# Tokens stored and loaded back by chunk, changed parameter and table code, and expert rows gathered into four buffers

## What is computed

```python
S = exp(dt_Lambda[..., None] * t - P_max)              # 128 heads, 64 states, 512 steps
Wc = Wc * (exp(dt_Lambda_neg) - 1) * conj(x) / (x * conj(x) + EPS)   # x = den * Lam
h = einsum("chn,hnl->chl", Wc, S).real                 # the tokenizer: 16 x 128 x 512
h = concat(cls_tok, h)
h = h + scan_layer(layernorm(h))    # z = x W_in; gated recurrence both ways; W_out; layer norm
h = h + moe_ffn0(layernorm(h))      # 8 experts, top 2, hidden 256, and a shared expert of 512
h = h + gla_layer(layernorm(h))     # gated linear attention, 16 heads
h = h + moe_ffn1(layernorm(h))      # 8 experts, top 2, hidden 352, and a shared expert of 1408
```

## Time and profile before

| | us |
|---|---|
| median of 3 runs | 1627.94 |
| lowest, highest | 1627.8, 1629.62 |
| the profiled execution, its own time | 1627.72 |
| its span, first to last instruction | 1625.9 |
| PE busy, in the span | 1398.0 |
| DVE busy | 841.7 |
| POOL busy | 476.5 |
| ACT busy | 368.8 |

### The profile page before, as it was taken

How to read it: one execution, slowest core, us unless ns; L and a number is a source line. 1 busy time by engine, 2 the same in 40 slices (tenths; PEclk the granted TensorE clock), 3 DMA queues, 4 the chain that set the end, 5 groups by cost and what they waited for, 6 DMA issues and landing times.

```text
span 1625.9 us, 21254 instructions
## 1 busy us (share of the span) xinstructions
PE 1398.0 (86%) x6461; PEld 1083.6 (67%) x6462; DVE 841.7 (52%) x1730; ACT 368.8 (23%) x703; POOL 476.5 (29%) x350
## 2 busy tenths in 40 slices
PE   0193685999899999379999899999999988989996
PEld 0193333888544444136777588888888877878885
DVE  7895468755322222464567775555555532333332
ACT  1011204211111111142222312332333111212221
POOL 0390502053134444100111025533333112333332
PEclk9999887999999999778999999999999999999998
DMA  2267002501665555610000303666666587666433
GB/s 54 56 103 161 0 0 76 179 21 33 248 174 97 90 91 94 193 30 1 1 1 1 137 20 127 207 213 221 206 207 203 225 323 241 183 179 175 84 71 45
DMA packets 90596, 193.87 MB, mean 119 GB/s; under 512 B 30128, under 2 KB 34096, under 8 KB 87216
## 3 DMA queue, kind: packets, MB, share of 16 engines
q1 hardware_dynamic: 70448, 151.19, 28.4%
q0 software_dynamic: 20096, 42.02, 14.3%
HBM read 112.24 MB, written 77.87 MB: 117 GB/s over the span
## 4 chain that ended last, share of the span: by engine, by line
PE 74%; DVE 12%; DMA 8%; issue 2%; ACT 1%; SPq 1%; POOL 1%; POOLq 0%; DVEq 0%; ACTq 0%
PE ps L1449 21%; PE ps L1509 19%; PE ps L1570 9%; PE ps L1970 6%; DMA out<-moe_scratch 6%; PE ps L1596 4%; PE ps L401 3%; PE ps L1543 2%; DVE held L454 2%; PE ps L510 2%; PE ps L1942 1%; PE ps L729 1%; PE ps L730 1%; PE ps L1584 1%; PE ps L1995 1%
## 5 line engine op out<-in xcount | busy, mean ns | idle before, releaser
L1509 PE MATMUL ps<-moe_rounded 128*128 128x384 f32 (+2 forms) x1800 | 374.1, 350 | 0.0
L1509 PEld LDWEIGHTS ps<-moe_rounded 128*128 128x128 f32 x1800 | 325.7, 188 | 33.1
L1226 DVE SCALAR_TENSOR_TENSOR held<-ps,moe_scratch,held 128x512 f32<-128x512 f32 (+1 forms) x255 | 187.5, 747 | 178.5 <-PE ps L1449 178.3
L1449 PE MATMUL ps<-moe_expert_parts,moe_rows_parts 128*128 (+1 forms) x1320 | 261.8, 352 | 4.5 <-DVE moe_rows_parts L1234 3.1
L1449 PE MATMUL ps<-moe_rounded 128*128 128x512 f32 (+3 forms) x885 | 239.6, 391 | 8.2 <-DVE moe_rounded L1208 6.1
L1449 PEld LDWEIGHTS ps<-moe_expert_parts,moe_rows_parts 128*128 128x128 f32 (+1 forms) x1320 | 222.2, 192 | 18.6 <-issue 5.3
L1449 PEld LDWEIGHTS ps<-moe_rounded 128*128 128x128 f32 (+2 forms) x885 | 145.3, 170 | 46.7 <-DVE moe_rounded L1208 8.1
L1240 DVE TENSOR_TENSOR moe_scratch<-moe_scratch,ps 128x256 f32<-128x256 f32 (+1 forms) x80 | 37.6, 470 | 230.4 <-ACT moe_scratch L1430 230.4
L1570 PE MATMUL ps<-moe_experts,moe_scratch 128*128 x320 | 145.9, 599 | 1.7 <-ACT moe_scratch L1416 1.1
L1327 POOL TENSOR_TENSOR moe_split_parts<-moe_scratch,moe_split_parts 128x704 fp32r<-128x704 f32 (+2 forms) x48 | 88.3, 1845 | 173.9 <-ACT moe_split_parts L1405 173.8
L1246 DVE TENSOR_SCALAR moe_scratch<-ps,moe_scratch 128x512 f32<-128x512 f32 x80 | 60.0, 751 | 130.6 <-PE ps L1596 56.8
(11 more groups left out here) (295 smaller groups left out, 1630.8 us busy)
## 6 DMA issues: line engine op xcount, KB each, us to landing
moe_expert_parts<-expert_parts SPq DMA_DIRECT2D x8, 3840.0 KB, 14.5
expert_parts<-moe_split_parts SPq DMA_DIRECT2D x32, 704.0 KB, 3.7
moe_scratch<-in_ffn_gate_up SPq DMA_DIRECT2D x32, 352.0 KB, 4.7
xn_rows<-moe_xn SPq DMA_DIRECT2D x2, 4096.0 KB, 12.8
moe_experts<-in_ffn_gate_up SPq DMA_DIRECT2D x8, 1024.0 KB, 11.6
expert_parts<-moe_split_parts SPq DMA_DIRECT2D x8, 1024.0 KB, 4.7
moe_scratch<-in_ffn_sh_gate_up SPq DMA_DIRECT2D x15, 512.0 KB, 3.4
tokens<-sb SPq DMA_DIRECT2D x64, 64.0 KB, 2.3
```

Of the source, the lines that this page charges most:

```text
L1226: v.scalar_tensor_tensor(out=hb[0:rows, t, :], in0=ps[0:rows, ADDED[t % 3], :], scalar=sg[0:rows, t:t + 1], in1=hb[0:rows, t, :], op0=ALU. ...
L1449: mm = t.matmul(out, lhs(k, x), rhs(k, y), start=(k == 0 and i == 0), stop=(k == ks - 1 and i == 2))
L1509: mm = t.matmul(unit_banks(u, m)[j], weights(k, x, j), xT[y][:, k, unit_cols(m)], start=(k == 0 and i == 0), stop=(k == KD - 1 and i == 2))
```

## The change

- Front: one DMA brings all parameters, laid out on the host as 128x186. The loads of x and the scan layer's weights are issued ahead of all else, GpSimd's two `memset`s (`zero`) too.
- The arguments of the sine are made once, and the cosine's come from them by one instruction (`cosine_args`, with a bias of pi/2 in ScalarE). The coefficient steps are merged over numerator and denominator.
- GpSimd waits for the eight table DMAs of the first group only; the four factor DMAs are issued behind `tabr` 2 and behind these eight. The fourth group is spread behind the stores of chunk 0.
- `tokens` is laid out by head. A chunk is stored by two DMAs of 256 KB, one for each bank, and read back by one DMA of 512 KB into the 16 partitions of its heads (`load_chunk`); the last chunk is read back in four quarters. The layer norm starts when all chunks and the first quarter of the last are there.
- ScalarE makes `xn` for the odd tiles (L712 of the new kernel), and the projection of quarter 0, 1, 2 and 3 follows tile 3, 9, 14 and 16.
- Experts: four buffers each for gathered rows and for results; two of each lie in `hb`, so that the first use of these waits for the stores of h (`hst`). `LAG` is 6, a gather waits for the tile four before it, and the loop is over four tiles.

```diff
-    def sync(sp):
...
+    def loads(sp):
+        sp.dma_start(params, d["tok_params"]).then_inc(par_in, 16)
         for w, k in ((wre, 0), (wim, 1)):
             for half in (LO, HI):
...
+        def tables(k):
             frm = LO if k < 2 else HI
             for to, lo, hi in ((R1, re[:, 0], re[:, 0]), (D1, re[:, 1], im[:, 1]), (I1, im[:, 0], im[:, 0]), (D2, ni2, re[:, 1])):
                 spread(to, LO, lo, frm, k, t_in[k])
                 spread(to, HI, hi, frm, k, t_in[k])
-            if k == 0:
-                sp.wait_ge(tabr, 2)
+
...
+        def store(k, b):
+            sp.wait_ge(evac, 2 * k + b + 1)
+            sp.dma_start(h0v[:, k * HC + b * H8:k * HC + (b + 1) * H8, :],
+                         ob[:, k % 2, b * QC:(b + 1) * QC].rearrange("p (h j) -> p h j", j=TJ)).then_inc(stored[k % 2], 16)
+
+        def load_chunk(k):
+
+            sp.wait_ge(stored[k % 2], 16 * 2 * (k // 2 + 1))
+            heads = slice(k * HC, (k + 1) * HC)
+            sp.dma_start(hb[heads, 0:NB, :], rows_of(heads, 0, NB)).then_inc(h_in[0], 16)
...
+        tables(0)
+        sp.wait_ge(tabr, 2)
+        sp.wait_ge(t_in[0], 8 * 16)
+        factors(0)
+        for k in range(1, 3):
+            tables(k)
+            factors(k)
+        last = NHC - 1
         for k in range(NHC):
-            u = k % 2
-            sp.wait_ge(evac, 2 * k + 2)
...
-                             ob[i * NB:(i + 1) * NB, u, :].rearrange("c (h j) -> c h j", j=TJ)).then_inc(stored[u], 16)
-            if k == NHC // 2 + 1:
-                load(LO)
-        load(HI)
+            store(k, 0)
+            if k >= 2:
+                load_chunk(k - 2)
+            store(k, 1)
+            if k == 0:
+                tables(3)
+                factors(3)
+        load_chunk(last - 1)
+        sp.wait_ge(stored[last % 2], 16 * NHC)
+        heads = slice(last * HC, NH)
+        for g in range(NQ):
+            sp.dma_start(hb[heads, 4 * g:4 * g + 4, :], rows_of(heads, 4 * g, 4 * g + 4)).then_inc(h_in[g], 16)
...
-        def args(out, mm, mmk, kk, ph):
-
-            c.link(v.tensor_scalar(out, mmk, ph, MAGIC, ALU.add, ALU.add))
-            c.link(v.scalar_tensor_tensor(out=out, in0=out, scalar=-MAGIC, in1=mm, op0=ALU.add, op1=ALU.subtract))
-            c.link(v.scalar_tensor_tensor(out=out, in0=out, scalar=-ph, in1=kk, op0=ALU.add, op1=ALU.subtract))
-            return v.tensor_scalar(out, out, -0.5, 0.5, ALU.max, ALU.min)
+        def sine_args(out, mm, mmk, kk):
+
+            c.link(v.tensor_scalar(out, mmk, MAGIC, -MAGIC, ALU.add, ALU.add))
+            c.link(v.tensor_tensor(out, out, mm, ALU.subtract))
+            c.link(v.tensor_tensor(out, out, kk, ALU.subtract))
+            c.link(v.tensor_scalar(out, out, -0.5, 0.5, ALU.max, ALU.min))
 
...
+        def cosine_args(out, x):
+
+            return v.scalar_tensor_tensor(out=out, in0=x, scalar=0.25, in1=x, op0=ALU.is_gt, op1=ALU.subtract)
...
+        c.put(v.scalar_tensor_tensor(out=xr, in0=dr, scalar=lam[:, 0:1], in1=w2[:, 0], op0=ALU.mult, op1=ALU.subtract))
+        c.link(v.scalar_tensor_tensor(out=xi, in0=dr, scalar=lam[:, 1:2], in1=w2[:, 1], op0=ALU.mult, op1=ALU.add))
+        c.put(v.tensor_tensor(w2, x2, x2, ALU.mult))
+        c.put(v.tensor_tensor(cc, num, bc(xr.unsqueeze(1), 1, 2), ALU.mult))
...
             if u == 0:
-                g.wait_ge(t_in[k // 2], 12 * 16)
+                g.wait_ge(t_in[k // 2], 12 * 16 if k else 8 * 16)
...
+                    v.wait_ge(h_in[t // NQ], H_LOADED[t // NQ])
                 norm.take_stats(v, hb, t)
                 c.n += 1
             norm.solve_some(v, c, tiles)
+            cols = slice(tiles[0], tiles[-1] + 1)
+            c.put(v.scalar_tensor_tensor(out=nmr[:, cols], in0=norm.mv[:, cols, 0], scalar=-1.0, in1=norm.rstd[:, cols], op0=ALU.mult, op1=ALU.mult))
+            solved.append(c.base + c.n)
             for t in tiles:
-                norm.apply(v, xn, hb, t).then_inc(xr, 1)
+                if t not in BY_SCALAR:
+                    norm.apply(v, xn, hb, t).then_inc(xr, 1)
 
...
-            s.wait_ge(turned, n + 1)
-            turned_out(s, ps[:, TURN_BANKS[n % 4], :], xnT, n).then_inc(tev, 1)
+        for k, tiles in enumerate(GROUPS):
+            s.wait_ge(norm.sem, solved[k])
+            for t in tiles:
+                if t in BY_SCALAR:
+                    s.activation(xn[:, t, :], hb[:, t, :], ACT.Identity, bias=nmr[:, t:t + 1], scale=norm.rstd[:, t:t + 1]).then_inc(xa, 1)
+            for n in tiles:
+                s.wait_ge(turned, n + 1)
...
             if n >= 4:
                 t.wait_ge(tev, n - 3)
             turn_tile(t, ps[:, TURN_BANKS[n % 4], :], xn, n, ident).then_inc(turned, 1)
-            if n == 7:
-                project(slice(0, QC), QC, 2)
+            if n in AFTER:
+                quarter(AFTER[n])
         t.wait_ge(tev, T)
-        for q in range(1, NQ):
-            project(slice(q * QC, (q + 1) * QC), QC, 2 + q)
         project(slice(NCOL, NTOK), NB, 6)
...
+    g_in, G0 = g.rows_gathered, 16 * (NTILE // DEEP) if split_w else 0
+    xg_of = [xg[:, 0], xg[:, 1], hb[:, 0, :], hb[:, 1, :]]
+    ey_of = [ey[:, 0], ey[:, 1], hb[:, 2, :], hb[:, 3, :]]
     tx, txr = sem(name + "_rows_turned"), sem(name + "_rowsT_ready")
     eg, esr, ehr = sem(name + "_e_gate_up"), sem(name + "_e_silu"), sem(name + "_e_hidden")
...
-        def out_rows(t, u):
+        def out_rows(t, x):
+            u = x % 2
             v.wait_ge(ed, D0 + t + 1)
-            if not early(t):
-                v.wait_ge(yst[u], 16 * halves(t))
-            v.tensor_scalar(ey[:, u], ps[:, 6 + u, :], idx[:, bass.ds(t, 1), 1], None, ALU.mult).then_inc(eyr, 1)
+            if not (isinstance(t, int) and t < DEEP):
+                v.wait_ge(yst[u], 16 * halves(t - 2))
+            elif t == 2:
+                v.wait_ge(hst, 16 * (NQ + 1))
+            v.tensor_scalar(ey_of[x], ps[:, 6 + u, :], idx[:, bass.ds(t, 1), 1], None, ALU.mult).then_inc(eyr, 1)
 
...
-    LAG = 4
+    LAG = 6
...
+        def four(i):
+            for k in range(1, DEEP + 1):
+                body(DEEP * i + k, k % DEEP)
+
+        looped(eng, (NTILE - 2) // DEEP, four)
+        for t in range((NTILE - 2) // DEEP * DEEP + 1, NTILE - 1):
+            body(t, t % DEEP)
...
-                if t >= 2:
-                    p.wait_ge(tx, t - 1)
-                p.indirect_dma_start(out=xg[:, t % 2], out_offset=None, in_=xd,
-                                     in_offset=bass.IndirectOffsetOnAxis(ap=idx_u[:, t, 0:1], axis=0)).then_inc(g_in[t % 2], 16)
+                if t >= DEEP:
+                    p.wait_ge(tx, t - DEEP + 1)
+                elif t == 2:
+                    p.wait_ge(hst, 16 * (NQ + 1))
+                p.indirect_dma_start(out=xg_of[t % DEEP], out_offset=None, in_=xd,
+                                     in_offset=bass.IndirectOffsetOnAxis(ap=idx_u[:, t, 0:1], axis=0)).then_inc(g_in[t % DEEP], 16)
             if t >= LAG:
...
+DEEP = 4
...
-        h0 = nc.dram_tensor("tokens", (NB, NH, D), F32).ap()
+        h0 = nc.dram_tensor("tokens", (NH, NB * TI, TJ), F32).ap()
```

188 lines of the change are left out of this document (96 added, 92 removed).

## The result

The changed kernel takes 1603.57 us (1602.61 to 1604.48) where the kernel before took 1628.24, the median of four runs on the same chip: ratio 0.9847, 95% interval 0.983 to 0.9864, so it is 1.5% faster, clear of the spread between runs. The forecast was 1610 with a range of 1596 to 1624. The profiled execution's span went from 1625.9 to 1601.3, -24.6 us, where the sum had -18.0.

What follows compares the result with a forecast made beforehand. TensorE held 74% of the chain that ended last, so the gain had to come from the rest: -1.4 + 1.6 - 5.2 - 13 = -18.0 on 1627.72 us gave 1609.7, say 1610, with a range of 1596 to 1624.

Steps and rivals of the forecast that it cites:

- The front: Start until the coefficient tables are done: 61.6 against 62.98 us, -1.4, with 11.8 lost to six GpSimd products.
- GpSimd hardly disturbs the coefficients: Rival in the front: GpSimd's early products cost VectorE's chain little, 11.8 us more gain, 1598 us; chance 0.14.
- Stores and loads: Tokenizer's end: SyncE's queue bounds it, first statistics at 107.1 + 7.25 L = 144.8 us against 143.2, +1.6.
- L: Tokenizer's loads back: time of one 512 KB load into 16 partitions, taken as 5.2 us.
- L = 2.6: Rival on loads back: as fast as into 64 partitions, evacuations the bound, statistics at 136.6, time 1602; chance 0.15.
- statistics at 137: Sign at the tokenizer's end: first statistics at 137 or past 160 us would mean a wrong L.
- The slower rival: Loads back take 10.3 us each, in proportion to partitions; statistics wait until 181.8, time 1647; chance 0.09.
- Layer norm: First statistics through the first projection: 22.2 + 1.8 + 6.8 + 1.8 + 3.6 + 0.9 = 37.1 us against 42.3, -5.2.
- The rest of the program is untouched: 0: Everything outside the front, loads back, layer norm and expert tiles was forecast to change by 0.
- ffn1: Second expert layer's tiles: -12.3 to result 22, -3.2 from fewer loop edges, 2.5 given back for gathers: -13 us.
- the buffers give nothing: Rival in ffn1: the scatter chain is the bound and moves with the weight loads, time 1623; chance 0.07.
- fully decoupled: Rival in ffn1: gathers and scatters no longer hold each other, 8.1 us more gain, 1602 us; chance 0.10.

Runs made afterwards that it cites:

- e1: Changed kernel, but GpSimd waits for all twelve spreads of the first group, so its first products start behind the coefficients; 1593.29 us, ratio 0.9799 to the kernel before.
- e2: Changed kernel, but GpSimd makes only chunk 0's three products early and chunk 1's wait for the coefficient tables; 1597.17 us, ratio 0.9826 to the kernel before.
- e3: Changed kernel, but all seven whole-chunk loads into 16 partitions follow the last stores; 1629.4 us, ratio 1.0026 to the kernel before.
- e4: Changed kernel, but four loads of 1 MB into 128 partitions behind the last stores replace all chunk loads; 1600.39 us, ratio 0.9852 to the kernel before.
- e6: Changed kernel with the old projection order: quarter 0 behind tile 7, quarters 1 to 3 behind the last tile; 1609.04 us, ratio 0.9883 to the kernel before.
- e9: Changed kernel, but GpSimd adds beta to h only when VectorE's two scans have ended; 1601.83 us, ratio 0.9842 to the kernel before.
- e12: Changed kernel with products behind tables, wide loads at the end, adds behind scans, eight result buffers with varied lag; 1590.38 us, ratio 0.9773 to before.
- e7: Changed kernel with two buffers for gathered rows and results, a two-tile loop and lag four, as before, in both expert layers; 1615.03 us, ratio 0.9912 to before.
- e8: Changed kernel with eight result buffers, a loop over eight tiles and scatters eight tiles behind; 1613.59 us, ratio 0.9914 to the kernel before.

## Why the prediction came out as it did

**The front: -1.4 forecast, -2.9 measured, for the reason given.** Every link was near: first instruction 2.86 (3.5), first spread 34.30 (35.0), GpSimd's first product 40.82 (41.7), tables at 60.06 (61.6). e1 and e2 show that the price of 11.8 us for six products was 11.1. The rival that GpSimd hardly disturbs the coefficients is wrong, since e1 differs from the changed kernel by that alone and its tables end at 48.94. The Trainium skill's rule in "SBUF — State Buffer", section "Who interferes with whom", of an exclusive lock for a whole instruction, agrees with the VectorE rows of 1.86 to 2.45 us. So does the add of 5.49 us beside a scan.

**Stores and loads: the step that failed.** "I take 5.2" for L was 4.6 to 4.7 (e3), and the 2.5 taken for a store was too much too: store and load of a chunk together took 6.0 to 6.3 us, not 7.7, so a store cost some 1.6. Under 7.11 the queue is not the bound, so 107.1 + 7.25 L does not set the statistics; with L = 4.7 it would give 141.2, and they stood at 137.51. What set them is the case that the forecast gave to L = 2.6 only: the last evacuation, and then the last store and load, 10.8 us where 8.4 was reckoned. The last store and the quarter load each had a narrow load in the queue ahead: the store landed 0.8 us behind the load of chunk 5, the quarter 1.2 behind that of chunk 6. In e4, which has neither, the same stretch took 7.6. The sign "statistics at 137", which was to mean a wrong L, came true, but the bound was wrong more than L. The sum has a slip here too: 144.8 is a time from the start of the span, so +1.6 holds the gain of the tables already, and adding -1.4 to it counts that twice. Counted once, the forecast would have been 1611.1, and the stretch up to the statistics, -5.7 measured, was forecast at +1.6 and not at the +0.2 of the table's two rows. The slower rival (L = 10.3) falls with e3: it would have needed loads at half of 111 GB/s. In the Trainium skill, "SBUF — State Buffer", section "Door 1: The DMA port swizzle (why [64,N] ≈ [32,N])" gives 16 partitions half the reach of 64; 111 GB/s to the 203 of the earlier trace rows agrees.

**Layer norm: -5.2 forecast, -7.5 measured.** Up to the last applies it was right, 21.8 for 22.2. Behind them the sum had 1.8 + 6.8 + 1.8 + 3.6 + 0.9 = 14.9 and it took 13.0: ScalarE's passes (159.44 to 161.67) and TensorE's turning of the last group's first four tiles (160.05 to 161.96) didn't follow one another, but ran beside each other, and from 162.29 on TensorE hardly stood.

**The rest of the scan layer: 0 forecast, +2.2 measured.** "The rest of the program is untouched: 0" was the overlooked step. The adds of GpSimd started at 161.84 and ended at 186.91, inside the second scan, where before they had ended (170.47 + 20.84 = 191.3) before the scans began at 193.93. The shorter layer norm pushed them together, and the two scans lost 1.57 us by it. From the first gate to ffn0's result 0 it is 256.3 to 256.6 us in e6, e9 and e12, whose scans meet no add, and 256.7 before; in the changed kernel and the eight others with both scans disturbed it is 257.3 to 258.9. So the adds account for the step, 1.6 us of it in the scans' own rows and the rest not traced.

**ffn1: -13 forecast, -13.1 measured.** The size is partly luck, as runs with the same code differ by up to 5.7 us here. Result 22 gained 9.6 us, where 12.3 were forecast and 2.5 given back for late gathers, 9.8: VectorE's waits for scatters were as foreseen, and one gather still came 3.67 late. The remaining 3.5 lie in the 17 later tiles, 3.2 forecast, where TensorE stood ahead of a tile to be turned with nothing to wait for 16 times (9.6 us) before and 7 times (4.7 us) now: fewer loop edges. e7 gives 11.6 of it back by undoing this part alone, so the rival "the buffers give nothing" is out, and 272.7 us, where "fully decoupled" would have given 264.7, rules out the other. e8 is the decoupled case, 262.3 us, and shows why it is not worth having by itself.

In sum the front's stages were 8 us better than forecast and the stage of the scans 2 worse, and the rest within 1. The total is off by 6.6 of 24.6, and it lies in the front.

## What to carry to other kernels

- A GpSimd instruction that is moved forward beside a chain of small linked VectorE instructions on SBUF costs that chain its whole length: 1.85 us for each product here. Let it start behind the chain if nobody waits for it; the wait of e1 is one changed number and was worth 11.1 us at the first statistics and 7.8 in the whole.
- When a stage gets shorter, list what ran just ahead of the next one on the neighbour engine. Here adds that had ended 2.6 us before the scans ran into them, and the last two cost the scans 1.57 us.
- In a serial chain of DMAs that the next stage waits for, the first issue and the last decide. More buffers let the compute engines run ahead of it, and moved the wait to the end of the layer.

## What was not expected of the hardware

- A load into 16 partitions runs at 111 GB/s with the DMA share at 0.98, and seven of them into different partitions don't overlap, while 128 partitions take 426.
- A long scan of VectorE and an add of GpSimd don't share: an add of 1.25 us that began beside a scan took 5.49 and ended behind it, and a scan of 4.45 that began beside an add took 5.13 or 5.34.
- A scatter of 128 rows takes some 5.6 us from its issue to the next one's, and 11.7 to 16.4 while weights in DMAs of 3.8 MB are on their way, four to six times in each kernel; in the changed kernel the first of ffn1 took 20.0, for 14.0 before.
